# A state space stage whose B and C rows share two PSUM banks in turn, with log(1+e) as four quadratics, one place for all mixture ends, two Silu blocks and one subtraction on GpSimd

## The reference

```python
def _mamba_forward(x, W_in, conv_w, conv_b, W_x, w_dt, b_dt, A_log, D, W_out):
    xz = x @ W_in
    xc, z = jnp.split(xz, 2, axis=-1)
    xp = jnp.pad(xc, ((0, 0), (D_CONV - 1, 0), (0, 0)))
    xconv = conv_b
    for k in range(D_CONV):
        xconv = xconv + xp[:, k:k + Ll, :] * conv_w[:, k]
    xs = jax.nn.silu(xconv)
    A = -jnp.exp(A_log)
    x_dbl = xs @ W_x
    ...
    delta = jax.nn.softplus(d_raw * w_dt + b_dt)
    def step(h, inp):
        dt, b, c, xt = inp
        At = jnp.exp(dt[..., None] * A)
        h = At * h + (dt * xt)[..., None] * b[:, None, :]
        y = jnp.einsum('bdn,bn->bd', h, c)
        return (h, y)
    ...
    y = jnp.swapaxes(ys, 0, 1) + xs * D
    y = y * jax.nn.silu(z)
    return y @ W_out
```

## Time and profile before

| what | value |
|---|---|
| median of 3 runs | 3344.35 us (3341.31 to 3345.94) |
| the profiled execution | 3349.86 us, its span 3348.1 us, mean granted clock 0.833 |
| busy in the span | PE 2475.0 us (74%), DVE 2246.2 (67%), ACT 1495.1 (45%), POOL 1146.9 (34%) |
| the state space stage | from 1624.97 us to 2397.59 us of the span |

### The profile page before, as it was taken

One profiled execution on the slowest core, in us unless ns is written; L12 is line 12 of the kernel. 1 busy time (PEld: TensorE's weight loads), 2 busy tenths in 40 slices (PEclk: granted clock), 3 DMA queues, 4 the chain that ended last, 5 costly groups with the idle time before them and its releaser, 6 DMA issues. The chain is left out here.

```text
span 3348.1 us, 49628 instructions
## 1 busy us (share of the span) xinstructions
PE 2475.0 (74%) x17670; PEld 1227.2 (37%) x17678; DVE 2246.2 (67%) x4538; ACT 1495.1 (45%) x2911; POOL 1146.9 (34%) x1172
## 2 busy tenths in 40 slices
PE   3999997784888885656467777767525937989986
PEld 1333333442444443546322222222214922333334
DVE  4888867884667663642388878888642247888844
ACT  1787771120455562323244543444311214777752
POOL 3222204442212101332345555555573433232001
PEclk9999997776799996768778776777757967999988
DMA  5121100001112111007500000000016932222000
GB/s 164 33 39 22 38 1 0 1 1 19 32 34 46 26 25 57 22 23 263 169 0 0 0 1 0 0 0 0 6 34 199 314 102 42 40 37 35 21 4 23
DMA packets 129159, 157.04 MB, mean 47 GB/s; under 512 B 18001, under 2 KB 110289, under 8 KB 128305
## 3 DMA queue, kind: packets, MB, share of 16 engines
q1 hardware_dynamic: 119248, 139.91, 16.0%
q0 software_dynamic: 6592, 13.56, 1.2%
q10 hardware_dynamic: 3072, 0.40, 0.1%
HBM read 95.56 MB, written 25.59 MB: 36 GB/s over the span
## 5 line engine op out<-in xcount | busy, mean ns | idle before, releaser
L422 DVE TENSOR_REDUCE a_mx<-banks 128x1 f32<-128x512 f32 (+3 forms) x1536 | 882.1, 617 | 256.5 <-PE banks L762 125.7
L633 ACT ACTIVATE a_prob<-banks 128x512 f32<-128x512 f32 (+3 forms) x1536 | 774.1, 545 | 381.2 <-PE banks L785 160.8
L785 PE MATMUL banks<-a_Qs,a_Ks 64*128 64x512 bf16 (+3 forms) x1536 | 511.9, 366 | 49.0 <-ACT a_prob L633 42.1
L762 PE MATMUL banks<-a_Ks,a_Qs 63*128 63x512 bf16 (+3 forms) x1536 | 503.4, 375 | 46.9 <-DVE a_mx L422 32.8
L813 PE MATMUL banks<-a_prob,a_vaug 128*32 128x256 f32 (+2 forms) x5632 | 444.4, 388 | 0.8 <-ACT a_prob L633 0.5
L2062 PE MATMUL banks<-m_hc,kc 128*128 128x512 f32 x512 | 341.5, 767 | 117.7 <-POOL m_hc L1938 98.8
L1938 POOL TENSOR_TENSOR m_hc<-m_h,m_cs 128x512 f32<-128x512 f32 x256 | 328.0, 1298 | 285.2 <-DVE m_h L1802 275.3
L1985 ACT ACTIVATE banks<-m_dt,acoef 128x512 f32<-128x512 f32 x256 | 175.8, 690 | 297.1 <-DVE m_h L1802 296.8
L1802 DVE TENSOR_TENSOR_SCAN m_h<-banks,m_u 128x512 f32<-128x512 f32 x256 | 301.4, 1208 | 0.0
L762 PEld LDWEIGHTS banks<-a_Ks,a_Qs 63*128 63x128 bf16 x1536 | 126.6, 95 | 408.2 <-DVE a_mx L422 213.4
L1787 DVE TENSOR_TENSOR m_u<-m_dtx,banks 128x1024 f32<-128x1024 f32 x128 | 155.2, 1213 | 105.2 <-PE banks L2043 102.6
(11 more groups left out here) (404 smaller groups left out, 4596.6 us busy)
## 6 DMA issues: line engine op xcount, KB each, us to landing
c_wbuf<-in_w2e SPq DMA_DIRECT2D x71, 512.0 KB
b_wbuf<-in_w1e SPq DMA_DIRECT2D x39, 578.0 KB
a_Ks<-a_parts SPq DMA_DIRECT2D x288, 64.0 KB
a_Qs<-a_parts SPq DMA_DIRECT2D x288, 64.0 KB
rows_in<-in_unused SPq DMA_DIRECT2D x1, 4579.5 KB, 16.8
c_yb<-rows_in SPq DMA_DIRECT2D x71, 64.5 KB
a_mixed_in<-rows_back SPq DMA_DIRECT2D x16, 256.0 KB, 4.0
a_Qs<-a_negm ACTq DMA_DIRECT2D x192, 2.0 KB
```

The lines of the kernel that those rows point to most:

```text
L422: dve.tensor_reduce(mx[:, g % 2, col:col + 1], M[:, k % 3, 0:keys[j]], AX.X, ALU.max).then_inc(S("max_read"), 1)
L633: act.activation(prob[:, n % 8, first_query[kt]:T], Sc[:, n % 2, first_query[kt]:T], ACT.Exp, scale=scale).then_inc(S("exped"), 1)
L762: i = pe.matmul(M[:, k % 3, 0:keys[j]], Qs[lo:lo + LAST, b % 4, pair, j * P:(j + 1) * P], Ks[lo:lo + LAST, b % 4, pair, 0:keys[j]], start= ...
L785: i = pe.matmul(Sc[:, n % 2, q0:T], Ks[lo:lo + HALF, b % 4, pair, kt * P:(kt + 1) * P], Qs[lo:lo + HALF, b % 4, pair, q0:T], start=True, s ...
```

## The change

It has six parts, all in `mamba_all`:

1. The two banks `Bs` and `Cs` become `R`, used in turn: B of step k lies in `R[k % 2]`, C of step k in the other one. C of step k is spread after `u` of step k - 1, and B of step k + 1 is spread right after the copy of C of step k, ahead of `u` of step k.
2. log(1 + e) = e times a polynomial of degree 8, factored into four quadratics c (e - r)^2 + c i^2. ScalarE makes the four squares (`sq`, Square with a bias from `shift`), VectorE multiplies them up in four scalar_tensor_tensor instructions, each with two inputs in SBUF. e lies in `mag` instead of `X`.
3. All mixture ends but that of batch 0 are planned at the start of the first fill, one every 3.0, with the norm on ScalarE (Identity with scale and bias) and two more small steps on GpSimd; g2 and the sum are VectorE's for all eight.
4. Silu of xs and Silu of z are two blocks, some steps apart, with a table load on either side of each.
5. The last part of `G` moves from VectorE to GpSimd.
6. `LEAD` is 70 instead of 66, and the planned times within a fill are set anew; the convolution's eight matmuls start nearer to the turn, the projection to B and C comes ahead of that to dt.

```diff
-            STEP, LEAD = 4.0, 66.0
+            STEP, LEAD = 4.0, 70.0
+            POLY, SOFT = (53.5, 55.5, 56.8, 58.9), 60.2
...
-                Y, Bs, Cs, A, X = flat[:, 0:2, :], flat[:, 2, :], flat[:, 3, :], flat[:, 4:6, :], flat[:, 6:8, :]
+                Y, R, A, X = flat[:, 0:2, :], flat[:, 2:4, :], flat[:, 4:6, :], flat[:, 6:8, :]
...
+                    return 1.0 if b == 0 else begin(0) + 2.0 + 3.0 * (b - 1)
...
+                def scalar_end(act, b):
+                    g, own = back_in[:, b], small1[:, b % 2]
+                    yield end_at(b) + 4.0
+                    act.wait_ge(S("end_shift"), b + 1)
+                    for j in range(NT):
+                        i = act.activation(g[:, j, :], g[:, j, :], ACT.Identity, bias=own[:, 3, j:j + 1], scale=own[:, 1, j:j + 1])
+                    i.then_inc(S("end_scaled"), 1)
...
-                    for n, factor in enumerate(LOG1P[::-1]):
-                        yield t + 40.0 + 1.3 * n
...
-                            i = dve.scalar_tensor_tensor(q[:, :, :], q[:, :, :], factor, X[:, :, :], ALU.add, ALU.mult)
...
+                    for n in range(NQ):
+                        yield t + POLY[n]
+                        dve.wait_ge(S("squared"), NQ * b + n + 1)
...
+                        i = dve.scalar_tensor_tensor(q[:, :, :], sq[:, n], QUADS[n][2], q[:, :, :] if n else mag[:, :, :],
+                                                     ALU.add, ALU.mult)
...
+                    yield t + 59.8
+                    gp.wait_ge(S("mid_part"), b + 1)
...
+                    gp.tensor_tensor(G[64:96, b % 2, :], rest[64:96, :], mid[64:96, :],
+                                     ALU.subtract).then_inc(S("parted"), 1)
...
+                    act.activation(mag[:, :, :], mag[:, :, :], ACT.Exp, scale=-1.0).then_inc(S("e_ready"), 1)
+                    for n in range(NQ):
+                        if n in (1, 3):
+                            yield t + (53.2 if n == 1 else 57.2)
...
+                        act.activation(sq[:, n], mag[:, :, :], ACT.Square, bias=shift[:, n:n + 1],
+                                       scale=QUADS[n][0]).then_inc(S("squared"), 1)
...
+                def tensor_scan(pe):
+                    def spread_b(k):
+                        b, n = divmod(k, DS)
+                        if n == 0:
+                            pe.wait_ge(S("parted"), b + 1)
+                        if k:
+                            pe.wait_ge(S("c_taken"), k)
+                        pe.matmul(R[:, k % 2, :], kb("sel32", 96)[:, n:n + 1].broadcast_to([96, P]), G[:, b % 2, :],
+                                  start=True, stop=True).then_inc(S("b_spread"), 1)
...
+                        yield at(k) - 5.6
+                        if k:
+                            pe.wait_ge(S("u_ready"), k)
+                        pe.matmul(R[:, (k + 1) % 2, :], kb("sel32", 96)[:, DS + n:DS + n + 1].broadcast_to([96, P]),
+                                  G[:, b % 2, :], start=True, stop=True).then_inc(S("c_spread"), 1)
+                        if k < DS * B - 1:
+                            yield at(k) - 4.2
+                            spread_b(k + 1)
```

More of the change, by code:

```diff
@@ L1817, in end_at @@
                 def end_at(b):
-                    return (1.0 + 7.0 * b, 6.0 + 10.5 * (b > 0) + 7.0 * b - 7.0 * (b > 0)) if b < 4 else (begin(b) - 14.0, begin(b) - 9.0)
+                    return 1.0 if b == 0 else begin(0) + 2.0 + 3.0 * (b - 1)
                 def vector_end(dve, b):
-                    g, (early, late) = back_in[:, b], end_at(b)
-                    yield early
+                    g = back_in[:, b]
+                    yield end_at(b)
                     dve.wait_ge(S("end_loaded_%d" % b), 48)
@@ L1837, in vector_end @@
                     i.then_inc(S("end_moments"), 1)
[L1838 to L1847, removed]
-                        dve.tensor_tensor(xres[:, b], g, xres[:, b], ALU.add).then_inc(S("x_ready"), 1)
+                    yield end_at(b) + 5.5
+                    dve.wait_ge(S("end_scaled"), b + 1)
+                    link(dve, dve.tensor_tensor(g, g, rep(wc("g2")), ALU.mult))
+                    dve.wait_ge(S("end_based"), b + 1)
+                    dve.tensor_tensor(xres[:, b], g, xres[:, b], ALU.add).then_inc(S("x_ready"), 1)
                 def gpsimd_end(gp, b):
-                    g, (early, late) = back_in[:, b], end_at(b)
-                    yield early + 0.2
+                    own = small1[:, b % 2]
+                    yield end_at(b) - 0.3
                     gp.wait_ge(S("end_loaded_%d" % b), 48)
                     gp.tensor_tensor(xres[:, b], xres[:, b], rep(wc("be2")), ALU.add).then_inc(S("end_based"), 1)
-                    yield early + 2.5
+                    yield end_at(b) + 2.5
                     gp.wait_ge(S("end_moments"), b + 1)
@@ L2086, in tensor_batch @@
                     for c in range(NCH):
-                        yield t + 31.5 + 0.8 * c
+                        yield t + 31.1 + 1.9 * c
                         pe.wait_ge(S("silu"), 4 * b + c + 1)
-                        pe.matmul(X[:, 1 - c, :], wc("win")[:, DI + c * P:DI + (c + 1) * P], hT[:, DC - 1:DC - 1 + T],
+                        pe.matmul(X[:, c, :], wc("win")[:, DI + c * P:DI + (c + 1) * P], hT[:, DC - 1:DC - 1 + T],
                                   start=True, stop=True).then_inc(S("in_projected"), 1)
-                    yield t + 33.5
+                    yield t + 39.0
                     pe.wait_ge(S("silu"), 4 * b + 3)
+                    for c in range(NCH):
+                        i = pe.matmul(X[0:96, 0, :], wc("wxp")[:, c * 96:(c + 1) * 96], xs[:, b % 2, c, :],
+                                      start=c == 0, stop=c == NCH - 1)
+                    i.then_inc(S("bc_projected"), 1)
+                    yield t + 41.0
+                    pe.wait_ge(S("silu"), 4 * b + 4)
                     for c in range(NCH):
@@ L2096, in tensor_batch @@
                     i.then_inc(S("dt_projected"), 1)
-                    yield t + 35.0
-                    pe.wait_ge(S("silu"), 4 * b + 4)
-                    for c in range(NCH):
-                        i = pe.matmul(X[0:96, 0, :], wc("wxp")[:, c * 96:(c + 1) * 96], xs[:, b % 2, c, :],
-                                      start=c == 0, stop=c == NCH - 1)
-                    i.then_inc(S("bc_projected"), 1)
                     yield at(DS * (b + 1)) + 9.0
```

150 lines of the change are left out of this document (75 added, 75 removed).

## The result

The changed kernel takes 3206.94 us (median of 4 runs, 3202.05 to 3216.96), the one before 3345.14 beside it: ratio 0.959, 95% interval 0.9564 to 0.9616, so 138 us less. Forecast were 3223 us, within 3187 to 3264. The profiled execution took 3202.05 us (span 3200.2, granted clock 0.859 over the whole kernel; 0.833 before).

What follows compares the result with a forecast made beforehand. VectorE's work and its waits for the B matmul bound the kernel. Work 63.6 plus idle 9.1 make 72.7 us a batch instead of 90.1: -122, first fill +2, last batch -1, giving 3223 us, range 3187 to 3264.

Steps and rivals of the forecast that it cites:

- my own forecast: Whole kernel: 7 to 12 us of idle time a batch, 3209 to 3244 us, likeliest 3223; chance 0.55.
- the rival in which nearly all idle time goes: Seven batches: VectorE keeps only 3 to 6 us idle a batch, 3180 to 3201 us; chance 0.20.
- Banks: Before `u`: B needs only the copy of C, so the 99.7 us of idle time behind B should nearly go.
- VectorE's work: Seven batches: VectorE's busy time falls from 521.75 by 76.5 to 445.2 us, 63.6 a batch.
- Idle time: VectorE, a batch: 9.1 us from Silus 2.5, polynomial 2.6, convolution 0.8, boundary 2.5, contention for SBUF interfaces 0.7.
- boundary: Between batches: sums still wait and TensorE leaves the polynomial at half clock; 2.5 of some 6 us stay idle.
- The 1.4 in the polynomial: First quadratic waits 1.4 us behind Relus, Exp and first square, 3.4 us in a row on ScalarE.
- First fill: Before the first `u`: Silus start 2 to 6 us later, squares save 5, `G` costs 1; +2 us taken.
- its cover: `G` on GpSimd: GpSimd, busy 55% of the stretch, hides the move; without that, 1.3 us a batch.
- The rule against the change: Quadratics: two SBUF inputs contend with GpSimd, but mostly GpSimd waits; 0.7 us a batch allowed.
- Table loads: ScalarE's Silus: two more a batch, counted in the blocks; by the skill's drain estimate, 19 us more.
- "The waits only change engine": Rival, seven batches: stalls move between engines, VectorE keeps 13 to 16 us idle a batch, 3250 to 3268 us; chance 0.22.

Runs made afterwards that it cites:

- The two experiments: Only the banks undone in the changed kernel: 3366.99 us, ratio 1.0031; only the banks changed on the kernel before: 3321.38 us, ratio 0.9909.
- The late ends: Changed kernel with the mixture ends of batches 4 to 7 planned in the batches again: 3209.75 us, ratio 0.9582.
- a Horner step: Changed kernel with Horner's nine VectorE instructions for squares and quadratics: e in SBUF 3283.97 us, e in a PSUM bank 3260.45 us.
- the displaced quadratic: First quadratic in the changed kernel with ScalarE's polynomial blocks smaller and earlier: 3203.93 us, ratio 0.9570.
- the tuned version: Changed kernel with ScalarE's polynomial blocks smaller and earlier, quadratics behind scans, residual addition and time-step projection moved: 3192.53 us, ratio 0.9542.

## Why the prediction was right, and where its sizes were off

- **Where the time fell.** 3206.94 us lies in the range, but just below the 3209 to 3244 of my own forecast and above the 3180 to 3201 of the rival in which nearly all idle time goes. The mechanism is the forecast's; VectorE's idle time and its work were both set somewhat too high.
- **Banks: right, and worth more than the sum says.** The idle time before `u` fell as stated. That B now only needs the copy of C is in the groups: 74.1 of its matmul's 74.6 us of idle time end with that copy. What the banks are worth the sum had too low: it lets 46 us of idle time go in the seven batches, and without the banks they take 143 us more. The two experiments show that neither they nor the rest do it alone.
- **VectorE's work: 440.70 against 445.2.** A quadratic took 1207 to 1225 ns, as the row it was priced by. I had left out the aggregates of the four ends, 1.5 us, and of a batch's own statistics that now fall outside the stretch, 1.2; scans and `u` are 1.3 shorter.
- **Idle time: 7.3 us a batch (51.4 by seven) against 9.1.** By the groups, which overlap a little: Silus 3.0 (2.5 forecast); polynomial 2.6 (2.6, in the two places named, 1.38 and 1.20); convolution 0.5 (0.8), all that waits behind B, of which more than half is in the first batch; boundary 1.1 (2.5: only the residual addition waits; the mis-sized term); contention 0 on VectorE (0.7), because it was GpSimd that paid, 4.42 us for two products.
- **The 1.4 in the polynomial.** The prediction gives no working for it, and a block of 3.4 less a slack of 2.6 would be 0.8. The timeline does: Relus, Exp and square take 3.57 us from 0.10 after the start of two scans that take 2.33, so the first quadratic is 1.3 late. That the size was met is in part luck.
- **Sum of the seven batches: -138.9 against -122.** Idle time (1.8 us a batch) and work (0.6) are the difference, 17 in all.
- **First fill +2.0 (+2), last batch -3.0 (-1).** The first Silu comes 45.7 us after the stage's first instruction instead of 38.7, 7.0 later (2 to 6 forecast), and from there to the first `u` it is 24.0 instead of 29.0. The prediction's pieces (2 to 6, -5, +1) add up to -2 to +2, not to its -4 to +6; the +2 was their upper end, and was met because the Silu was later than forecast. The late ends (above) show the trade: four ends fewer make the fill 13.4 shorter and the batches 15.0 longer.
- **`G` on GpSimd: its cover held.** It took 1150 ns there, 1800 on VectorE; returning it cost 2.0 us a batch.
- **The rule against the change.** The contention exists (scans 1200 to 1786 ns, a Horner step 1202 to 1444, the displaced quadratic 1225 to 1696), as the Trainium skill, GPSIMD Engine Reference, 8. Key points, has it. It cost VectorE nothing here (quadratics 1207 to 1225 ns): they start as scans end, ahead of the product, and GpSimd had the time.
- **Table loads.** 28 of them show 0.5 us of idle time ahead in all, and the work behind follows at once. The drain of 1.38 us beside each load, in the Trainium skill, ScalarE: Activation LUTs, What ACT_TABLE_LOAD costs, isn't seen here.
- **Rivals.** "The waits only change engine" is what the banks alone do (72 of 99 us), and it is wrong for the whole change only because the new order and the squares came with them. TensorE's clock rose, 0.76 to 0.89, with 83 us less busy time. Without the banks it rose too, to 0.83, and nothing was gained. That the rise helped the time by itself wasn't tried; with 3.4 us waiting for B, there is little left for it to help. In the tuned version, at 0.94, that wait is 10.9 all the same.
